# A four-layer graph network on one core: degrees by additions of whole blocks, and h of layer 1 turned and multiplied between the neighbour sums of layer 0

## The reference

```
x  = x + LN(h @ W_self.T + mean_of_neighbours(h) @ W_neigh.T + bias) * gamma + beta      # layer 0
# layer 1, twice: g = h @ W ; deg = segment_sum(w, dst) ; dinv = where(deg > 0, rsqrt(deg), 0)
#                 out[v] = b + sum over (u->v) of dinv[u] * w * dinv[v] * g[u]
x  = x + l2_normalised(gcn(relu(gcn(h, W1, b1)), W2, b2))                                # layer 1
```

## Time and profile before

| | us |
|---|---|
| median of 3 runs | 1444.81 (1444.22 to 1449.42) |
| profiled execution, time | 1448.26 |
| profiled execution, span | 1446.5 |
| TensorE busy | 1266.0 (88%) |
| VectorE busy | 1021.7 (71%) |
| GpSimd busy | 712.4 (49%) |
| ScalarE busy | 577.6 (40%) |

### The profile page before, as it was taken

The page is one execution under the profiler, slowest core; times in us unless marked ns, Lnnn a source line. Parts: engine busy times, 40 slices in busy tenths (PEclk is TensorE's granted clock), DMA queues, the critical chain, the costliest instruction groups (busy, mean ns, idle before and its releaser), DMA issues.

```text
span 1446.5 us, 20064 instructions
## 1 busy us (share of the span) xinstructions
PE 1266.0 (88%) x4424; PEld 739.3 (51%) x4424; DVE 1021.7 (71%) x1900; ACT 577.6 (40%) x1462; POOL 712.4 (49%) x873
## 2 busy tenths in 40 slices
PE   4859899078898898959998989999999889997998
PEld 2534444033333333428875444544554578885775
DVE  8798253078899899850267268888898898888432
ACT  0211311066666620112011168888888723334210
POOL 0577777767787735766672166666666100000000
PEclk9989999589999998979999999999999899998999
DMA  8932512020000044443222367777776200002220
GB/s 336 335 127 67 196 53 75 23 103 19 17 26 17 10 169 167 124 155 101 87 90 98 131 208 218 232 226 222 230 223 217 57 1 0 1 0 84 73 91 35
DMA packets 87239, 167.90 MB, mean 116 GB/s; under 512 B 16108, under 2 KB 44654, under 8 KB 84628
## 3 DMA queue, kind: packets, MB, share of 16 engines
q1 hardware_dynamic: 59044, 102.19, 21.0%
q0 software_dynamic: 25472, 59.97, 13.7%
q10 hardware_dynamic: 2672, 5.11, 1.2%
HBM read 115.97 MB, written 51.25 MB: 116 GB/s over the span
## 4 chain that ended last, share of the span: by engine, by line
PE 44%; issue 17%; DVE 12%; DMA 12%; POOL 10%; DVEq 2%; POOLq 1%; ACT 0%; ACTq 0%; SPq 0%
DMA arena<-p_rows,gidx 9%; POOL cell_rows L690 9%; PE pb L1090 7%; PE pb L1206 6%; PE pb L1198 6%; PE pb L1385 5%; PE pb L1288 3%; PE pb L1356 3%; PE pb L1358 3%; PE pb L1357 3%; DVE arena L1632 2%; DMA cell_rows<-tiles,gidx 2%; PE pb L1172 2%; DVE arena L1437 1%; DVE arena L1616 1%
## 5 line engine op out<-in xcount | busy, mean ns | idle before, releaser
L801 POOL DMA_INDIRECT arena<-p_rows,gidx x184 | 189.7, 1031 | 66.9 <-issue 60.4
L736 POOL DMA_INDIRECT dst_rows<-ering,gidx x168 | 167.7, 998 | 102.5 <-issue 73.6
L690 POOL DMA_INDIRECT cell_rows<-tiles,gidx x168 | 168.3, 1002 | 67.9 <-issue 40.2
L1288 PE MATMUL pb<-arena 128*128 128x512 f32 x368 | 190.1, 599 | 5.4 <-ACT arena L961 5.4
L1632 DVE TENSOR_TENSOR arena<-pb,arena 128x384 f32 x272 | 151.8, 558 | 26.5 <-PE pb L1172 24.2
L1090 PE MATMUL pb<-ws,tiles 128*128 128x512 f32 (+1 forms) x360 | 146.5, 555 | 12.3 <-ACT tiles L823 12.3
L1741 DVE TENSOR_TENSOR arena<-pb,arena 128x512 f32<-128x512 f32 x184 | 124.3, 685 | 40.1 <-DMA arena<-p_rows,gidx 38.1
L1172 PE MATMUL pb<-arena 128*128 128x384 f32 x272 | 105.6, 515 | 45.5 <-POOL arena L743 45.4
L864 ACT ACTIVATE arena<-iota,free 128x128 f32<-128x128 f32 x272 | 94.3, 393 | 112.6 <-PE pb L1172 69.7
L1172 PE MATMUL pb<-tiles,arena 128*128 128x384 f32 x272 | 103.3, 506 | 19.7 <-DVE arena L1632 18.3
L1090 PEld LDWEIGHTS pb<-ws,tiles 128*128 128x128 f32 x360 | 67.3, 195 | 69.5 <-issue 53.5
(11 more groups left out here) (285 smaller groups left out, 2378.2 us busy)
## 6 DMA issues: line engine op xcount, KB each, us to landing
dst_rows<-arena SPq DMA_DIRECT2D x6, 2046.0 KB, 17.5
ering<-in_edge_attr_dram SPq DMA_DIRECT2D x41, 256.0 KB, 3.0
arena<-adj SPq DMA_DIRECT2D x10, 640.0 KB, 4.0
arena<-dst_rows SPq DMA_DIRECT2D x24, 264.0 KB, 2.8
arena<-wt_gru SPq DMA_DIRECT2D x48, 128.0 KB
ws<-dst_rows SPq DMA_DIRECT2D x22, 264.0 KB, 2.8
arena<-in_x_dram SPq DMA_DIRECT2D x18, 256.0 KB, 9.0
arena<-in_L_gnn_W_hh_dram SPq DMA_DIRECT2D x3, 1024.0 KB, 20.3
```

The source lines that it names most:

```text
L690: nc.gpsimd.indirect_dma_start(cell_rows[:, :], bass.IndirectOffsetOnAxis(gidx[:, SPAN * a + k:SPAN * a + k + 1], 0), cring[:, a, k], None ...
L736: nc.gpsimd.indirect_dma_start(dst_rows[:, :], bass.IndirectOffsetOnAxis(gidx[:, k:k + 1], 0), ering[:, k, :], None).then_inc(e_scattered[ ...
L801: nc.gpsimd.indirect_dma_start(rows[:, k, :], None, p_rows[:, :], bass.IndirectOffsetOnAxis(gidx[:, k:k + 1], 0)).then_inc(g_landed[k], 16)
L1288: nc.tensor.matmul(e_bank(k)[:], erowT[:, k % 4], w1e_sb, start=True, stop=True).then_inc(edge_mm, 1)
```

## The change

- `degree(m, halves)` makes the partial degrees of a whole matrix by additions: for s = 1 to 9 it adds block s of five tiles at once (128x640 elements), the two halves of the tiles in turn, eighteen additions a matrix. An addition from s = 2 on waits for the one before the last. Both matrices are done straight behind the build.
- TensorE calls `degrees(0)` behind sum 1 and `degrees(1)` behind sum 2. `dinv` is made behind tile 1 (`DINV_AFTER = 1`, before 5), and a new semaphore `dinv_ready` says when.
- With `BEHIND = 4`, TensorE turns h(t - 4) behind sum t (from t = 4) and multiplies h(t - 5) with W1 behind that (from t = 5). Four turns and five products are left behind sum 9. ScalarE does the copies and scalings in its loop over t, behind relu t: `h1_turned(t - 4)`, `g1_scaled(t - 5)`.
- W1 lies in `spare` instead of `ws`, and ScalarE's queue loads it behind the first two ys tiles. The loads of W2, `wt_w1h` and the two biases stand behind ScalarE's loop, ahead of the copy h1T(6). W2 has its own semaphore `w2_there`, for which TensorE waits ahead of the first product with W2. ScalarE's wait for sum 9 stands ahead of relu 8 instead of relu 7.

```diff
@@ -258,7 +258,7 @@
         a1 = tiles[:, 2, :].rearrange("p (b f) -> p b f", b=2)
         a1T = tiles[:, 3, :].rearrange("p (b k n) -> p b k n", b=2, k=2)
         y1 = tiles[:, 0:2]
-        w1_sb = ws[:, 1].rearrange("p k f -> p (k f)")[:, 0:KT * DH].rearrange("p (k f) -> p k f", k=KT)
+        w1_sb = spare[:, 0:KT * DH].rearrange("p (k f) -> p k f", k=KT)
         w2_sb = ws[:, 1].rearrange("p k f -> p (k f)")[:, KT * DH:KT * DH + 2 * D].rearrange("p (k f) -> p k f", k=2)
         r2 = g.rearrange("p (t f) -> p t f", t=NT)
@@ -348,7 +348,7 @@
         block_done, block_added = sem("block_done"), sem("block_added")
         adj3_stored = [sem(f"adj3_stored{k}") for k in range(4)]
         adj3_loaded = [sem(f"adj3_loaded{k}") for k in range(2)]
-        deg_ready = sem("deg_ready")
+        deg_ready, dinv_ready = sem("deg_ready"), sem("dinv_ready")
         w2_loaded, m_stored = sem("w2_loaded"), sem("m_stored")
         b2_loaded, b2_ready = sem("b2_loaded"), sem("b2_ready")
         xe_loaded = [sem(f"xe_loaded{k}") for k in range(NT)]
@@ -362,7 +362,7 @@
         high3, low3 = sem("high3"), sem("low3")
         p_loaded, w3_loaded = sem("p_loaded"), sem("w3_loaded")
         h_ready = sem("h_ready")
-        w_loaded = sem("w_loaded")
+        w_loaded, w2_there = sem("w_loaded"), sem("w2_there")
         p_stored = [sem(f"p_stored{k}") for k in range(2)]
         g_ready = sem("g_ready")
         rows_passed = sem("rows_passed")
@@ -386,7 +386,8 @@
         blocks = [("w1h", 0), ("hh0", 0), ("hh1", 1), ("hh2", 2), ("w3", 0), ("ih0", 0), ("ih1", 1), ("ih2", 2),
                   ("neigh", 0), ("self", 0)]
         PREFIX2_AFTER = 5
-        DINV_AFTER = 5
+        DINV_AFTER = 1
+        BEHIND = 4
         act_jobs = []
         for n, (name, third) in enumerate(blocks):
             act_jobs += [("w", n, k) for k in range(5 if n == 0 else KT)]
@@ -394,8 +395,7 @@
                 act_jobs += [("m", third, k) for k in range(KT)] + [("c", third)]
         for t in range(NT + 1):
             act_jobs += ([("hsT", t)] if t < NT else []) + ([("zs", t - 1)] if t else [])
-        act_jobs += ["deg0", "deg1"]
-        h1_jobs = [("h1T", 0)]
+        h1_jobs = ["deg0", "deg1", ("h1T", 0)]
         for t in range(NT):
             h1_jobs += ([("h1T", t + 1)] if t + 1 < NT else []) + [("g1", t)]
         act_jobs += h1_jobs + [("a1T", t) for t in range(NT)]
@@ -892,6 +892,19 @@
             load_ys(0)
             load_ys(1)
+            nc.scalar.dma_start(w1_sb, w1_1.rearrange("(k p) f -> p k f", p=P)).then_inc(w_loaded, 16)
+
+            def h1_turned(t):
+                if t >= 2:
+                    act.wait_ge(for_act, A[("g1", t - 2)] + 1)
+                copy_job(("h1T", t), flat(hT[:, t % 2]))
+
+            def g1_scaled(t):
+                act.wait_ge(for_act, A[("g1", t)] + 1)
+                if t == 0:
+                    act.wait_ge(dinv_ready, 1)
+                nc.scalar.activation(g1[:, t], act_bank(("g1", t))[:, 0:DH], ACT.Copy,
+                                     scale=dinv[:, t:t + 1]).then_inc(act_read, 1)
             for t in range(NT):
                 if t == DINV_AFTER:
@@ -905,32 +918,27 @@
                 act.wait_ge(norm_ready, t + 1)
                 if t == 0:
                     act.wait_ge(adj3_stored[1], 16)
-                if t == 2 * KT - 1:
+                if t == 2 * KT:
                     act.wait_ge(for_dve, V[("y0", NT - 1)] + 1)
-                    nc.scalar.dma_start(w1_sb, w1_1.rearrange("(k p) f -> p k f", p=P)).then_inc(w_loaded, 16)
-                    nc.scalar.dma_start(w2_sb, w2_1.rearrange("(k p) f -> p k f", p=P)).then_inc(w_loaded, 16)
-                    act.wait_ge(wt_stored[0], 16 * 4)
-                    nc.scalar.dma_start(ws[:, 0].rearrange("p k f -> p (k f)"), wt_dram["w1h"]).then_inc(p_loaded, 16)
                 nc.scalar.activation(h[:, t], xs[:, t], ACT.Relu, bias=mv[:, t, 0:1], scale=rstd[:, t:t + 1]).then_inc(h_ready, 1)
                 if t == DINV_AFTER:
                     root("dinv", dinv[:])
-
-
-            for n, (kind, t) in enumerate(h1_jobs):
-                if n == len(h1_jobs) - 2:
-                    act.wait_ge(h_ready, NT)
-                    nc.scalar.dma_start(vec[:, 0, 0:DH], b1_1.rearrange("(a f) -> a f", a=1).to_broadcast([P, DH])
-                                        ).then_inc(vec_loaded, 16)
-                    nc.scalar.dma_start(vec[:, 1], b2_1.rearrange("(a f) -> a f", a=1).to_broadcast([P, D])
-                                        ).then_inc(vec_loaded, 16)
-                if kind == "g1":
-                    act.wait_ge(for_act, A[("g1", t)] + 1)
-                    nc.scalar.activation(g1[:, t], act_bank(("g1", t))[:, 0:DH], ACT.Copy,
-                                         scale=dinv[:, t:t + 1]).then_inc(act_read, 1)
-                else:
-                    if t >= 2:
-                        act.wait_ge(for_act, A[("g1", t - 2)] + 1)
-                    copy_job(("h1T", t), flat(hT[:, t % 2]))
+                if t >= BEHIND:
+                    h1_turned(t - BEHIND)
+                if t > BEHIND:
+                    g1_scaled(t - BEHIND - 1)
+
+            nc.scalar.dma_start(vec[:, 0, 0:DH], b1_1.rearrange("(a f) -> a f", a=1).to_broadcast([P, DH])).then_inc(vec_loaded, 16)
+            act.wait_ge(for_dve, V[("y0", NT - 1)] + 1)
+            act.wait_ge(norm_ready, NT)
+            nc.scalar.dma_start(w2_sb, w2_1.rearrange("(k p) f -> p k f", p=P)).then_inc(w2_there, 16)
+            act.wait_ge(wt_stored[0], 16 * 4)
+            nc.scalar.dma_start(ws[:, 0].rearrange("p k f -> p (k f)"), wt_dram["w1h"]).then_inc(p_loaded, 16)
+            nc.scalar.dma_start(vec[:, 1], b2_1.rearrange("(a f) -> a f", a=1).to_broadcast([P, D])).then_inc(vec_loaded, 16)
+            for t in range(NT - BEHIND, NT + 1):
+                if t < NT:
+                    h1_turned(t)
+                g1_scaled(t - 1)
             def turned1(t):
                 if t >= 2:
@@ -1223,23 +1231,30 @@
             pe.wait_ge(z_loaded[1], 16)
             for t in range(2):
                 sum0(t, range(2 * KT, NT))
-            sum0(2, range(NT))
-            sum0(3, range(NT))
             degrees(0)
-            for t in range(4, NT):
-                sum0(t, range(NT))
-                if t == 7:
-                    degrees(1)
-
-            pe.wait_ge(w_loaded, 32)
-            for t in range(NT):
+
+            def turn_h1(t):
                 pe.wait_ge(h_ready, t + 1)
                 turn_tile(("h1T", t), h[:, t])
-                if t:
-                    pe.wait_ge(act_read, A[("h1T", t - 1)] + 1)
-                    linear(("g1", t - 1), [(hT[:, (t - 1) % 2], w1_sb)], DH)
-            pe.wait_ge(act_read, A[("h1T", NT - 1)] + 1)
-            linear(("g1", NT - 1), [(hT[:, (NT - 1) % 2], w1_sb)], DH)
+
+            def linear_h1(t):
+                if t == 0:
+                    pe.wait_ge(w_loaded, 16)
+                pe.wait_ge(act_read, A[("h1T", t)] + 1)
+                linear(("g1", t), [(hT[:, t % 2], w1_sb)], DH)
+
+            for t in range(2, NT):
+                sum0(t, range(NT))
+                if t == 2:
+                    degrees(1)
+                if t >= BEHIND:
+                    turn_h1(t - BEHIND)
+                if t > BEHIND:
+                    linear_h1(t - BEHIND - 1)
+            for t in range(NT - BEHIND, NT + 1):
+                if t < NT:
+                    turn_h1(t)
+                linear_h1(t - 1)
             pe.wait_ge(act_read, A[("g1", NT - 1)] + 1)
             for t in range(NT):
                 sum_neighbours(("x1", t), matrix(1, t), g1, DH)
@@ -1252,6 +1267,7 @@
                 turn_tile(("a1T", t), a1[:, t % 2])
             turn1(0)
+            pe.wait_ge(w2_there, 16)
             for t in range(NT):
                 if t + 2 < NT:
                     sum_neighbours(("a1", t + 2), matrix(1, t + 2), x1, DH)
@@ -1651,17 +1667,26 @@
             turn(turns - 1, True)
             dve.wait_ge(block_added, CELL_CHUNKS)
-            def degree(m, t):
-                return nc.vector.tensor_reduce(deg_parts[:, m, t], adj3[:, m, t * NT:(t + 1) * NT].rearrange("p s d -> p d s"),
-                                               AX_X, ALU.add)
-
-            for t in range(NT):
-                ins = degree(0, t)
-            ins.then_inc(deg_ready, 1)
+            def degree(m, group):
+
+                for s in range(1, NT):
+                    for n, part in enumerate(group):
+                        blocks_of = adj3[:, m, part.start * NT:part.stop * NT].rearrange("p (t s) d -> p t s d", s=NT)
+                        total = deg_parts[:, m, part]
+                        if s > 1:
+                            dve.wait_ge(step, chain[0] - len(group) + 1)
+                        chain[0] += 1
+                        ins = vtt(total, blocks_of[:, :, 0] if s == 1 else total, blocks_of[:, :, s], ALU.add)
```

(15 more changed lines are left out.)

## The result

| | before | after |
|---|---|---|
| median of 12 runs each, one chip | 1448.65 us (1444.22 to 1452.64) | 1437.68 us (1435.28 to 1442.95) |
| ratio to before | | 0.9925, 95% interval 0.9911 to 0.994 |
| profiled execution, time and span | 1448.26 and 1446.5 | 1438.35 and 1436.6 |
| build's end to the first g1 sum | 146.5 us | 133.0 us |
| first g1 sum to the end | 773.3 us | 777.6 us |

The kernel became 0.75% faster, 11.0 us by the medians; 13.9 had been forecast, from a base of 1444.8. The time lies 0.2 us above the range.

The account below looks back on a forecast made before the run. No engine's total decides; the 146.5 us stage from build to first g1 sum holds 112.4 us of TensorE work plus waits and low clock. Starting g1 sums 13.9 us earlier takes 1444.8 to 1430.9, say 1431; range 1425.5 to 1437.5.

Parts of the forecast that it names:

- The wait for h1T(0): TensorE ahead of product 0: stands from 587.3 to 593.8, 6.5 us, until ScalarE copies h1T(0) behind relu 4.
- Rounds of 10.8 us without a wait: From tile 6 TensorE sets the pace: sum, turn and product take 10.8 us, the copies hidden with 3.5 us left.
- a low clock that costs 2.9 us: After TensorE's wait near 643 to 647: 2.9 us lost if the clock falls, which was left open.
- A call of degrees costs the sum behind it 1.8: On TensorE, the sum straight behind each call of degrees runs 1.8 us longer because the clock falls.
- The median 1444.8 becomes 1430.9: Whole kernel: the median of three runs, 1444.8 us, less the stage's 13.9 us gain, gives 1430.9.
- what comes after should move as a block: Behind the g1 sums: everything through the gathers shifts alike, nothing added, as GpSimd's 24.08 us pause is large enough.
- rival C: Behind the stage: its 14 us gain is given back at edge rows or gathers, 0 to 7 us remain; chance 0.11.
- A: In the stage: clock and queues are kinder, gain 17 to 19 us, 1426 to 1428 us; chance 0.15.
- B: In the stage: later first y0, low clock after the second wait or long issues, gain 8 to 10 us; chance 0.15.
- D: TensorE stays at the lower clock from the wait at 587 on, making the kernel slower, 1480 us; chance 0.03.
- E: Interleaving does nothing since h is never ready early, only the degrees count; no chance of its own, counted inside B.

Follow-up runs that it names:

- the late load experiment: The changed kernel with the load of W1 issued behind relu 0 instead of with the first two ys tiles: 1453.05 us, ratio 0.9865 to the kernel before.
- the second profile: The changed kernel run again unaltered, on another chip beside the kernel before: 1435.7 us against 1443.88, ratio 0.9933.
- The filled waits: The changed kernel with three idle products in each of TensorE's two waits ahead of the first p2 product: 1454.14 us against 1470.56, ratio 0.988.

## Why the prediction was right or wrong

**The stage was right.** The g1 sums were forecast at 659.3 and started at 659.02. Step by step, forecast and measured: an addition 0.78 us and 0.74 (13.3 for eighteen). The estimate of 0.82 from the formula of the Trainium skill ("VectorE: DVE Perf Modes", the errata section) was farther off: the starts of these additions lie 0.74 apart. Matrix 1 ready at 555.2 and 553.3. The last x tile landing at 556.3 and 556.8, with the late load experiment showing that W1's bytes are 1.5 us of VectorE's wait for it. The first y0 at 561.8 and 562.3. The wait for h1T(0) 6.5 us and 8.0, its product at 593.8 and 594.5 at half clock. Rounds of 10.8 us without a wait, and so they were from sum 6 to sum 9 (10.75 from one product with W1 to the next). Relu 9's end at 646.3 and 646.15, product 5 at 646.8 and 646.67, half clock behind it, which had been left open. That the end fits to 0.3 us is luck in part: the forecast took the middle between a low clock that costs 2.9 us and none; the clock did fall, and the product behind it took 3.56 us instead of 1.89, 1.7 more.

**One term of it was mis-sized, and another hid it.** "A call of degrees costs the sum behind it 1.8" held for degrees(0) (8.81 us) but not for degrees(1) (7.11). In the run with the changed kernel again neither cost anything (7.11 us each). The other way round, the first two sums were given 17.3 us and took 18.97, with the clock at 0.91 from 526 to 545 us; in the second profile they took 17.28. None of this moved the end: TensorE came sooner or later to a wait whose end VectorE and ScalarE set, which is why that wait measured 8.0 and 11.5 us, and not 6.5. The second profile's row:

```profile
594.79 3.75 PE L1098 MATMUL pb<-arena,tiles 128*128 128x256 f32 x8 [11.46 <-issue]
```

**What failed is the sum.** "The median 1444.8 becomes 1430.9" took the median of three runs for the level. The profiled execution stood at 1448.3, and twelve runs gave 1448.65. With that base the same 13.9 us give 1434.7, inside the range. Three more microseconds are missing, and they belong to the step "what comes after should move as a block". It moved by 14.2 at the g1 sums and 14.0 at p2, but by 12.5 at the first gather, 11.2 at the last and 9.9 at the end. Of these 4.3 us of the profile, 1.5 come between p2 and the gathers, and 1.3 of those are the low clock behind TensorE's waits ahead of p2: the first p2 product took 6.69 us against 5.40. The filled waits show that this stretch of the changed kernel has 2.8 us of it, and that of the kernel before already had some. It was the same in the second profile of the changed kernel (45.5). The rest, gathers 1.3, later stages 1.3 and 0.2 ahead of p2, was not there again: the second profile was 2.9 us shorter. But the loss is not the accident of one profile: beside that second profile the medians gave 8.2 us, while its stage was 13.0 shorter than in the first profile of the kernel before and 11.4 than in the second. What part of this is not the clock at p2 is open. It is rival C in a small part: something is given back later, but 3 us and not 7 or more, and the place was named wrongly. The scatter of the edge rows ended at 774 us, the clearing followed relu 9 of layer 2 at 782.7, so in the changed kernel the edge rows ended nothing. Why the low clock covers the first p2 product more often in kernels with the additions is open: it took over 6.6 us in five of their seven profiles of the first three sets and 3.70 in two, while the three without them had 5.40, 5.09 and, with the reductions back, 3.70. Filling both waits kept the clock up; no run showed which of the two, 2.6 and 3.0 us long, brings it down.

**The rivals.** A did not come. B's costs (dearer additions) did not come, its size nearly did: 11.0 against its 8 to 10. D had the clock at half only over the end of the long wait and product 0 (0.50 from 593 to 598, 0.83 in the 2 us behind) and again behind the wait at the end: in the rounds between, sums, turns and products ran at full clock (7.03, 0.60 and 1.89 us). E supposed that the interleaving might do nothing; it does worse than nothing in this place, and that was not among the rivals. The forecast walked the new order without pricing the same change without it. The expectation for that kernel, written once the result was known, had sum 9 near 620 and the g1 sums near 652; they came at 653.35.

## What to carry to other kernels

Work that is moved between the steps of a bound engine needs every helper of it moved as well: here a copy that stood behind a tile's relu in ScalarE's queue held TensorE for 8 us, though its input had been ready for 16. Price the half of a change without its other half; two parts that looked like one idea were worth 20 us and minus 7 of the stage. A long slack behind the change is used up by the next improvements: GpSimd's pause went from 24 us to 9 and then to nothing. And take a base from as many executions as there are, with the profiled one beside them: the median of three lay 3.8 us under that of twelve, more than half of the smallest gain that was to be told.

## What the hardware showed beyond expectation

- The same call of twenty one-column products (2.1 us) was followed by a sum of 8.81 us or of 7.11, with the granted clock falling or not, within one kernel and between two executions of it (8.81 and 7.11 in the first profile of the changed kernel, twice 7.11 in the second).
- In the stage of the change a TensorE wait of 3.43 us was followed by a product at half clock (3.56 us, where 1.89 is its length at full clock), nearly as one of 8.0 was (3.75), and waits of 3.84 and 4.04 as fully (3.78 and 3.75). One of 1.92 behind 8 us of full work saw the clock fall too, once, within the product. Behind waits of 0.42 to 1.00 us the products with W1 took 1.99 or 2.00 us.
- The first p2 product, with nothing filled, took from 3.70 to 6.77 us behind the same instructions; six idle products in the two waits ahead of it, with a granted clock of 1.00, made it 3.70 in both kernels that had them.
- The level of the same kernel was 1443.9, 1444.1 and 1448.65 us in three sets of runs and 1470.56 in a fourth, whose profile had the build's end 27 us later (553.4 against 526.7). Ratios to the kernel before, run beside, held: 0.9925 and 0.9933.
